# An attention-and-FFN block on one core: f32 transforms for two more pairs, doubled weights for the first pair, and a last output in two halves

## The reference

```python
# x: (16, 64, 512) f32, ctx: (16, 64, 512) f32; the FFN weights are f16
x = x + tanh(g_xattn) * autocorrelation(layernorm(x), ctx, ctx)
x = x + tanh(g_ffn)   * ffn(layernorm(x))

# autocorrelation, for every batch, head and feature, along the 64 tokens:
corr = ifft(fft(q) * conj(fft(k))).real      # 64 lags
w, idx = top_k(corr, 8); w = softmax(w)
out[t] = sum_i w[i] * v[min(idx[i] + t, 63)] # v shifted by the lag, clipped at the end

# ffn: 512 -> 1792 -> 512
h = silu(x @ W_gate.T) * (x @ W_up.T)
out = h @ W_down.T
```

## Time and profile before

| | |
|---|---|
| median of 3 runs | 218.98 us (218.32 to 219.37) |
| the profiled execution's own time | 218.67 us |
| its span, first to last instruction | 216.6 us |
| TensorE busy | 206.4 us, 95% |
| VectorE, ScalarE, GpSimd busy | 135.2, 145.1, 133.2 us |
| mean granted TensorE clock | 0.992 |

### The profile page before, as it was taken

The page is one execution under the profiler, slowest core; times in us unless marked ns, Lnnn a source line. Parts: engine busy times, 40 slices in busy tenths (PEclk is TensorE's granted clock), DMA queues, the critical chain, the costliest instruction groups (busy, mean ns, idle before and its releaser), DMA issues.

```text
span 216.6 us, 6596 instructions
## 1 busy us (share of the span) xinstructions
PE 206.4 (95%) x2686; PEld 147.4 (68%) x2686; DVE 135.2 (62%) x407; ACT 145.1 (67%) x225; POOL 133.2 (61%) x161
## 2 busy tenths in 40 slices
...
DMA packets 20061, 16.77 MB, mean 77 GB/s; under 512 B 15936, under 2 KB 16448, under 8 KB 19648
## 3 DMA queue, kind: packets, MB, share of 16 engines
...
HBM read 10.59 MB, written 2.10 MB: 59 GB/s over the span
## 4 chain that ended last, share of the span: by engine, by line
PE 87%; POOL 4%; DVE 3%; ACT 3%; issue 1%; DVEq 0%; ACTq 0%
PE psum L895 45%; PE psum L1067 22%; PE psum L878 6%; PE psum L1018 4%; PE psum L908 2%; PE psum L886 2%; PE psum L988 2%; ACT k_spec L647 1%; POOL mixed_lo L579 1%; POOL prod_lo L563 1%; ACT v_spec L639 1%; PE psum L1003 1%; POOL hid_lo L593 1%; PE psum L957 1%; PE psum L969 1%
## 5 line engine op out<-in xcount | busy, mean ns | idle before, releaser
L895 PE MATMUL psum<-xt_hi,wg 128*128 128x128 f16 (+1 forms) x504 | 55.0, 216 | 0.0
L895 PE MATMUL psum<-xt_lo,wg 128*128 128x128 f16 (+1 forms) x504 | 54.9, 215 | 0.0
L895 PE MATMUL psum<-xt_hi,wu 128*128 128x128 f16 (+1 forms) x504 | 53.9, 213 | 0.0
L895 PE MATMUL psum<-xt_lo,wu 128*128 128x128 f16 (+1 forms) x504 | 53.9, 213 | 0.0
L895 PEld LDWEIGHTS psum<-xt_hi,wg 128*128 128x128 f16 x504 | 46.0, 99 | 4.4 <-issue 2.5
L593 POOL TENSOR_TENSOR hid_lo<-hid,hid_hi 128x512 f16<-128x512 f32 (+2 forms) x32 | 33.0, 1038 | 24.5 <-ACT hid_hi L711 24.3
L895 PEld LDWEIGHTS psum<-xt_hi,wu 128*128 128x128 f16 x504 | 44.8, 98 | 4.1 <-issue 3.4
L895 PEld LDWEIGHTS psum<-xt_lo,wg 128*128 128x128 f16 x504 | 46.1, 99 | 0.6
L895 PEld LDWEIGHTS psum<-xt_lo,wu 128*128 128x128 f16 x504 | 45.1, 98 | 0.7
L704 ACT ACTIVATE act<-psum 128x512 f32<-128x512 f32 (+2 forms) x32 | 17.2, 537 | 39.1 <-PE psum L895 38.9
L1067 PE MATMUL psum<-wd,hid_hi 128*128 128x512 f16 x112 | 42.5, 379 | 0.0
...
## 6 DMA issues: line engine op xcount, KB each, us to landing
out<-x_sb SPq DMA_DIRECT2D x8, 256.0 KB, 2.5
...
x_sb<-x SPq DMA_DIRECT2D x4, 256.0 KB, 5.1
ctx_sb<-ctx SPq DMA_DIRECT2D x4, 256.0 KB, 5.1
ctx_sb<-ctx SPq DMA_DIRECT2D x1, 1024.0 KB, 20.0
...
```

What stands on the lines that cost most here:

```text
L895: last = nc.tensor.matmul(psum[:, bank, a * n:(a + 1) * n], w[:, k, m * P:(m + 1) * P], xt[:, e, k, tok], start=(k == 0 and part == 0), st ...
```

## The change

- `WHOLE_SPECTRA`, `WHOLE_LAGS`, `WHOLE_MIX` name the pairs that are worked in f32: spectra of pairs 0, 1 and 2 (before: 0 and 1), lags of pairs 0 and 1 (as before), mixtures of pairs 0, 1 and 2 (before: 0). For these steps the high and low parts and their steps fall away. The f32 mixing matrices of the packed form are two more blocks of the f32 table, with a load of their own behind the down weights.
- In pair 0 `scale` writes its weights twice side by side (VectorE, 512 columns for a batch instead of 256), so that the transposed weights stand on both halves of the partitions, and the two weight spectra of a batch (even and odd) use different row halves.
- In pair 0 the mask writes to `expo`, and weights of both batches take the whole of `probs`; pair 1's match therefore waits for pair 0's transposes.
- The load of ctx for pair 0 is issued by ScalarE instead of SyncE; the warm-up is 8 and 9 matmuls instead of 12 and 8.
- The last pair's down matmuls, output and store are done in two halves of 256 columns, in two PSUM banks.
- `ORDER` is written anew for all pairs. All turns stand on ScalarE in both kernels.

```diff
+WHOLE_SPECTRA = (0, 1, 2)
+WHOLE_LAGS = (0, 1)
+WHOLE_MIX = (0, 1, 2)
...
 ORDER = """
-warm:0 stats1:0 rstd1:0 kspec:0 q_norm:0 vspec:0 kcopy:0 kcopy:0.1 qspec:0 stats1:1 vcopy:0 vcopy:0.1 rstd1:1
-prod:0 prod:0.1 lags:0 gates:0 q_norm:1 scales:0 kspec:1 max:0 sub8:0 match:0 lags:0.1 warm:0.1 exp8:0 kcopy:1
-sub:0 total:0 exp:0 max:0.1 kcopy:1.1 mask:0 sub8:0.1 vcopy:1 scale:0 stats1:2 wt:0 w_hi:0 qspec:1 match:0.1
-rstd1:2 turn:1 wspec:0 sub:0.1 prod:1 exp8:0.1 exp:0.1 wspec:0.1 prod:1.1 turn:1.1 mask:0.1 lags:1 total:0.1
-q_norm:2 mix_prod:0 k_hi:2 scale:0.1 mix_prod:0.2 q_hi:2 wt:0.1 max:1 q_lo:2 mix:0 w_hi:0.1 turn:1.2 sub:1
-wspec:0.2 k_lo:2 match:1 exp:1 wspec:0.3 turn:1.3 mix:0.1 mix_prod:0.1 k_hi:3 sub8:1 k_lo:3 mix_prod:0.3
-kspec:2 exp8:1 residual:0 mix:0.2 kcopy:2 mix:0.3 vcopy:2 mask:1 rstd2:0 total:1 kcopy:2.1 residual:0.1
-scale:1 xn:0 xt:0 w_rows_hi:1 stats1:3 rstd2:0.1 qspec:2 x_hi:0 w_t:1 turn:2 x_lo:0 rstd1:3 prod:2 gate:0
...
+warm:0 stats1:0 rstd1:0 kspec:0 kcopy:0 q_norm:0 kcopy:0.1 qspec:0 stats1:1 vspec:0 prod:0 rstd1:1 prod:0.1
+lags:0 vcopy:0 q_norm:1 kspec:1 max:0 vcopy:0.1 sub8:0 lags:0.1 warm:0.1 sub:0 vcopy:1 stats1:2 kcopy:1
+match:0 rstd1:2 max:0.1 exp8:0 kcopy:1.1 total:0 sub:0.1 match:0.1 exp:0 qspec:1 turn:1 mask:0 sub8:0.1 prod:1
+exp8:0.1 gates:0 exp:0.1 prod:1.1 q_norm:2 total:0.1 lags:1 turn:1.1 mask:0.1 scale:0 scale:0.1 wt:0 max:1
+wt:0.1 w_hi:0 w_hi:0.1 wspec:0 sub:1 match:1 k_hi:3 wspec:0.1 turn:1.2 k_lo:3 mix_prod:0 kspec:2 exp:1
+mix_prod:0.2 turn:1.3 mix:0 scales:0 mix_prod:0.1 mix:0.1 mix_prod:0.3 sub8:1 mix:0.2 kcopy:2 residual:0
+mix:0.3 vcopy:2 mask:1 rstd2:0 kcopy:2.1 residual:0.1 exp8:1 qspec:2 xn:0 xt:0 total:1 rstd2:0.1 prod:2 x_hi:0
+x_lo:0 p_hi:2 scale:1 stats1:3 gate:0 xn:0.1 prod:2.1 p_lo:2 w_rows_hi:1 p_hi:2.1 w_t:1 xt:0.1 up:0 stats1:4
+tanh:0 p_lo:2.1 x_hi:0.1 silu:0 turn:2 rstd1:3 x_lo:0.1 lags:2 hid:0 turn:2.1 gate:0.1 w_rows_lo:1 max:2
+q_norm:3 up:0.1 w_t:1.1 k_hi:4 match:2 tanh:0.1 h_hi:0 gate:0.2 sub8:2 q_hi:3 h_lo:0 sub:2 silu:0.1 exp:2
+hid:0.1 exp8:2 kspec:3 tanh:0.2 mask:2 wspec:1 turn:2.2 total:2 up:0.2 scale:2 mix_prod:1 kcopy:3 mix_prod:1.1
...
-WARM_UP = ((12, 4), (8, 7))
+WARM_UP = ((8, 4), (9, 7))
...
-    w_whole = sb("w_whole", [L, 2, D])
+    w_whole = sb("w_whole", [P, 2, D])
...
+    def halves(p):
+
+        return (slice(0, D // 2), slice(D // 2, D)) if p == PAIRS - 1 else (slice(0, D),)
+
+    def down_psum(p, h):
+
+        cols = halves(p)[h]
+        return psum[:, down_bank(p) if h == 0 else w_bank(p, 0, 1), 0:cols.stop - cols.start]
...
-            load(ctx_sb, cv, 0, 1, ctx_loaded[0])
...
+            act.dma_start(ctx_sb[:, 0, :], ctx[0:P, :]).then_inc(ctx_loaded[0], 16)
...
-                if step == "scale" and mine:
-                    w = lag_cols(probs, p, n)
+                if step == "scale" and p == 0:
+                    to = twice(n)
...
-                    nc.vector.tensor_tensor(w, w, lag_sums(inv_total, p, n).unsqueeze(2).broadcast_to(w.shape),
+                    nc.vector.tensor_tensor(to, lag_cols(expo, p, n).unsqueeze(2).broadcast_to(to.shape),
...
-                    nc.tensor.matmul(psum[:, w_bank(p, m, b), :], consts32[0:L, forward32(("even", "odd")[m])],
-                                     w_whole[:, b, :], start=True, stop=True).then_inc(w_spectra, 1)
+                    for m, name in enumerate(("even", "odd")):
+                        last = nc.tensor.matmul(psum[:, w_bank(p, m, n), :], consts32[rows(m), forward32(name)],
+                                                w_whole[rows(m), n, :], start=True, stop=True)
...
+                if step == "mix" and p > 0 and p in WHOLE_MIX:
+                    pe.wait_ge(packed_mix_loaded, 16)
+                    pe.wait_ge(mixed_done, 4 * p + 3 + n)
+                    for b in range(2):
+                        last = nc.tensor.matmul(psum[rows(b), mix_bank(p, b), :], packed_mix32(n), mixed[:, 2 * n + b, :],
+                                                start=n == 0, stop=n == 1)
```

More of the change, by code:

```diff
@@ L176 @@
[L176 to L195, removed]
@@ new lines @@
+qspec:3 rstd2:1 down:0 prod:3 prod:3.1 p_hi:3 silu:0.3 p_hi:3.1 p_lo:3 wspec:2 hid:0.3 xn:1 down:0.1
+mix_prod:2 p_lo:3.1 x_rows_hi:1 mix_prod:2.1 q_norm:4 x_t:1 x_rows_lo:1 mix_prod:2.2 lags:3 h_hi:0.3
+mix_prod:2.3 turn:3 mix:2 h_lo:0.3 max:3 mix:2.1 k_hi:5 k_lo:4 x_t:1.1 q_hi:4 sub:3 down:0.2 match:3 exp:3
+k_lo:5 turn:3.1 down:0.3 q_lo:4 turn:3.2 kspec:4 out:0 gate:1 sub8:3 mask:3 exp8:3 kcopy:4 total:3 stats1:5
+scale:3 up:1 vcopy:4 residual:2 rstd1:5 w_rows_hi:3 kcopy:4.1 w_t:3 gate:1.1 stats1:6 rstd2:2 tanh:1 silu:1
@@ new lines @@
+w_rows_lo:3 qspec:4 tanh:1.1 up:1.1 xn:2 prod:4 rstd1:6 w_t:3.1 x_rows_hi:2 hid:1 p_hi:4 silu:1.1 store:0
+gate:1.2 h_hi:1 p_lo:4 prod:4.1 x_t:2 q_norm:5 hid:1.1 h_lo:1 p_hi:4.1 up:1.2 tanh:1.2 p_lo:4.1 turn:3.3
+silu:1.2 gate:1.3 hid:1.2 x_rows_lo:2 wspec:3 tanh:1.3 h_hi:1.1 silu:1.3 x_t:2.1 up:1.3 mix_prod:3 h_hi:1.2
+h_lo:1.1 lags:4 mix_prod:3.1 q_hi:5 down:1 q_norm:6 h_lo:1.2 max:4 m_hi:3 hid:1.3 m_hi:3.1 m_lo:3 down:1.1
+mix_prod:3.2 sub:4 m_hi:3.2 m_lo:3.1 match:4 turn:4 gate:2 exp:4 mix_prod:3.3 q_hi:6 kspec:5 sub8:4 h_hi:1.3
@@ new lines @@
+mask:4 exp8:4 h_lo:1.3 down:1.2 vcopy:5 total:4 m_lo:3.2 stats1:7 m_hi:3.3 up:2 q_lo:5 kcopy:5 kcopy:5.1
+m_lo:3.3 down:1.3 tanh:2 scale:4 mix:3 turn:4.1 out:1 mix:3.1 mix:3.2 q_lo:6 w_rows_hi:4 qspec:5 w_t:4
+gate:2.1 w_rows_lo:4 prod:5 silu:2 p_hi:5 hid:2 p_lo:5 up:2.1 tanh:2.1 prod:5.1 h_hi:2 w_t:4.1 silu:2.1
+p_hi:5.1 h_lo:2 gate:2.2 hid:2.1 k_hi:6 residual:3 p_lo:5.1 h_hi:2.1 up:2.2 tanh:2.2 turn:4.2 silu:2.2 rstd2:3
+lags:5 k_hi:7 hid:2.2 k_lo:6 gate:2.3 xn:3 max:5 x_rows_hi:3 h_lo:2.1 down:2 turn:4.3 match:5 x_t:3
@@ new lines @@
+silu:4 kcopy:7.1 mix:5 hid:4 mix:5.1 turn:6 mask:6 mix:5.2 qspec:7 residual:5 scale:6 h_hi:4 gate:4.1
+w_rows_hi:6 prod:7 rstd2:5 turn:6.1 w_t:6 up:4.1 tanh:4.1 h_lo:4 store:2 xn:5 silu:4.1 gate:4.2 w_rows_lo:6
+p_hi:7 hid:4.1 x_rows_hi:5 p_lo:7 w_t:6.1 up:4.2 tanh:4.2 h_hi:4.1 x_t:5 silu:4.2 turn:6.2 h_lo:4.1 prod:7.1
+gate:4.3 hid:4.2 p_hi:7.1 up:4.3 tanh:4.3 p_lo:7.1 turn:6.3 silu:4.3 wspec:6 hid:4.3 down:4 x_rows_lo:5
+h_hi:4.2 mix_prod:6 h_hi:4.3 mix_prod:6.1 m_hi:6 h_lo:4.2 x_t:5.1 lags:7 m_hi:6.1 down:4.1 h_lo:4.3 turn:7
```

182 lines of the change are left out of this document (98 added, 84 removed).

## The result

The changed kernel takes 219.19 us (median of 20 runs, 217.84 to 220.56) against 218.29 us for the kernel before (20 runs on the same chip): the ratio is 1.0052, with a 95% interval of 1.0030 to 1.0073. The forecast was 217.0 us, faster; it is 0.9 us slower. The profiled execution took 219.31 us, with a span of 217.1 and a mean granted clock of 0.976 (before: 218.67, 216.6 and 0.992).

The account below looks back on a forecast made before the run. TensorE bounds the kernel from the first gate matmul (work, stalls, half clock, tail); before it, mostly VectorE's queue. 218.67 + 0.65 (later front) + 0.8 (f32 mixtures) - 2.8 (stalls) - 0.35 (output) = 217.0 us, range 215.2 to 219.5.

Parts of the forecast that it names:

- Half clock: Pause ahead of the first gate matmul stays; its loss of about 1.2 us left as it is, bounds -1.2 and +0.5.
- Rival C: Clock falls earlier, at pair 1's lags, which take 4 us instead of 2.0; 220.4 us, chance 0.08.
- signs of being wrong: First gate after 33 us, second clock fall, GpSimd stalls over 1 us at 40 to 57, or new idle after 57.
- VectorE's chain: From first max to first residual: 15.0 us instead of 14.1, for wider scale steps, small scale operations and new waiting.
- Start of the queue: Fewer warm-ups and earlier ctx load, less slower spectrum and later normalisation: net -0.3 us, first max at 10.9 instead of 11.17.
- Doubled weights: Pair 0's weight spectra on two row halves: two times 0.86 us less on TensorE, worth nothing while it waits for VectorE.
- Stalls: TensorE's stalls around 43, 48 and 55 us, 3.1 us, go; 0.3 left for new ones: -2.8 us.
- Rival B: Stalls move rather than go, GpSimd's low halves holding TensorE at 40 to 57 us; 219.0 us, no change, chance 0.21.
- Mixtures in f32: Mixtures of pairs 1 and 2: about 1.72 us each instead of 1.31, +0.41 per pair, +0.8 in all.
- rival D: f32 column halves of the mixtures don't overlap; 220.4 us, chance 0.05.
- E: Full-depth f32 matmuls run at twice the f16 time, not four times, 0.86 us per mixture; 215.3 us, chance 0.01.
- Last output in halves: After the last matmul VectorE's output step takes 0.42 us instead of 0.75: -0.35 us; no gain taken for the half-size store.

Follow-up runs that it names:

- the first filled kernel: Changed kernel with zero matmuls (7, 8, 5 and 4) in its four early TensorE pauses; 216.8 us, ratio 0.9951 to the kernel before.
- single weights: Changed kernel with fillers in five pauses, pair 0's weights written once, both weight spectra on the first row half; 216.75 us, ratio 0.9948.
- the old-order run: Changed kernel's code in the order of the kernel before, 12 and 8 warm-ups, pair 2's spectra in f16 parts; 217.73 us, ratio 0.9964.
- filled against filled: Changed kernel with zero matmuls in four early pauses, 216.8 us, against the kernel before with 9 ahead of its first transpose, 217.46 us.
- the later fillers: Zero matmuls (8, 5 and 4) around the first transposes and before the first gate; alone in the changed kernel 217.26 us, ratio 0.9980.

## Why the prediction was wrong

The step that failed is the one under *Half clock*: "I leave that loss, about 1.2 us, as it is". It looked at one pause only. The runs showed two falls, and the text had the first of them among its rivals, as C. Two of its own signs of being wrong came: the first gate after 33 us (33.23), and a second fall.

- *Half clock.* After the first gate the loss is 180.91 - 179.06 = 1.85 us, against 181.89 - 180.82 = 1.07 before: +0.78 where 0 was forecast. Ahead of it, the fall from 20.49 us makes the weight spectra 1.2 us longer, and the mixture behind them late; VectorE's chain is 15.96 us instead of 15.35 in the same order at full clock: +0.61. Together +1.4, from 0.
- *Rival C* had the right mechanism and place and the wrong price. The fall came as pair 1's lags ended, so the lags kept their 2.0 us and max behind them waited 0.25, not 2; what was paid is in the spectra behind. It was priced at 3.4 (its terms, 2 and 1.3, give 3.3), with a chance of 0.08; its argument against, that nine warm-up matmuls had just run, did not hold: between them and the fall lay one query spectrum, 1.38 us without work and the lags.
- *VectorE's chain* was put at 15.0 us and takes 15.35 at full clock: +0.35. The waits for TensorE are 0.96 us in all; the 14.1 us of before had 0.36 of them in it (0.17 and 0.19), and 0.2 more was allowed.
- *Start of the queue.* The first max comes at 11.41 us, not 10.9: the first spectrum at the warm-up rate took 2.08 us, not 1.9 (1.7 and 0.17 of drain), and the query transform behind it waited another 1.49 for ScalarE, where the copy of k puts the normalisation 0.49 us later (7.35 instead of 6.86; 0.55 was forecast). This start varies by itself: 10.54 in the first filled kernel, where the same spectrum took 1.13.
- *Doubled weights* were "worth nothing" on the ground that TensorE waits for VectorE there. In the new order VectorE's residual waits for the mixture that stands behind these spectra, 1.30 us with single weights and 0.44 with doubled ones: doubling is worth 1.0 us of the chain.
- *Stalls.* -2.8 was right: first gate to last matmul falls by 1.76 at full clock, with the mixtures' +0.92 and the halves' 0.18 against it, so the stalls gave 2.86. GpSimd's busy time fell by 11.6 us for the 11.7 forecast. How the gain divides between the lighter GpSimd queue (at most 0.8 us of idle time by the old-order run) and the order is open. Rival B is out: TensorE has no idle time from 37.7 to 213 us.
- *Mixtures in f32.* 1.94 us drawn, 1.77 less the drain, against 1.31: +0.46 per pair for +0.41. Column halves overlap in f32 too, so rival D is out. E is out as well: the row of 1.94 us for eight instructions is near the 1.72 of the quarter rate, not 0.86. By the half rate of the Trainium skill (Perfetto Trace Analysis, section Engine Utilization), read per matmul, it would be 0.86; the trace does not agree.
- *Last output in halves.* In the span -0.64 for -0.35. The last output ends 0.80 us after the last matmul's start (214.94 - 214.14) instead of 1.17 (214.13 - 212.96): -0.37, though a half takes 0.48 us on VectorE where 0.42 was forecast. The other -0.27 is the store: the halves land in 1.7 and 1.8 us, the last full store of the kernel before in 2.0 (2.4 and 2.5 are medians of all full stores, after and before). The Trainium skill (DMA: Bandwidth & Descriptors, section Anatomy of one DMA, written for GpSimd's path) has about 2.0 us fixed and an estimated 0.3 for the halved bytes; the 0.2 to 0.3 us between these stores agree with the second, but this store, issued by SyncE, was quicker than that fixed part. In the times of the run with halves alone nothing of it is seen: by its interval the halves bring between 0.5 us less and 0.7 more, and the 0.46 that the trace leaves lies at the edge of that.

In sum: 2.16 for 0.65 at the first gate (0.5 start, 0.35 chain, 0.6 clock), -0.98 for -2.0 behind it (0.78 clock, 0.24 the rest, most of it the halves' 0.18 and the mixtures), -0.64 for -0.35 at the end, 0.1 outside the span. With the clock kept up by fillers the same kernel takes 216.8 us, 0.2 under the forecast; but the forecast had one fall's loss in it. At full clock the change brings 0.7 us filled against filled, and 1.4 by the few runs that kept the clock without the later fillers; VectorE's chain to the residual is 1.3 us longer in the new front than in the old one (15.35 against 14.08).
